# A transformer block on one core: second-matrix weights split once and kept, router steps respread, a prologue in another order

## The chip, the cores and the metric

The kernel runs on one core of one Trainium2 chip. The metric is the device time of one execution in microseconds (us); lower is better. The engines are TensorE (PE; its weight loads are listed as PEld), VectorE (DVE), ScalarE (ACT), GpSimd (POOL), and SyncE (SP), whose queue issues nearly all DMA transfers.

## What is computed

Eight batches of 512 tokens, width 512, all in float32: a cross-attention block, then a feed-forward block with a router.

```python
x = x + xattn(layernorm(x), ctx, ctx, mask, bias, Wq, bq, Wk, bk, Wv, bv, Wo, bo)   # 16 heads
z = layernorm(x)
...
r = clip(layernorm(z, ln_g, ln_b) @ router_W.T + router_b, -10, 10)     # 256 columns
phi, idx = top_k(softplus(r), 8)
Z = phi / (sum(phi) + 1e-6) * tanh(sum(phi))
h_lat = einsum('nd,nkd->nk', z, unit_rows(raw_U)[idx])
dyn = einsum('nk,nkd->nd', h_lat * Z, unit_rows(raw_V)[idx]) * gamma
static = gelu(z @ W1.T) @ W2.T                                          # 512 -> 2048 -> 512
x = x + static + dyn
```

## The kernel before

Three stages follow one another: `project` (projections), `attend` (attention), and `blend` (output projection, router, feed-forward). The change touches `blend` alone, which takes the second half of the time.

**Arithmetic.** A float32 matrix product is made of three passes of TensorE on rounded halves: high·high, high·low, low·high. So each operand needs a "high" copy (a rounding copy) and a "low" one (the operand less its high copy). The first matrix, W1, is loaded ready-made from a buffer in DRAM (`wf_d`). The second, W2, is loaded raw for each batch again, 16 blocks of 128x512: ScalarE makes the high half (`weight_high`, L1761) and GpSimd the low half (`weight_low`, L1369). GELU outputs are split by VectorE (`gelu_high`, L1601) and GpSimd (`gelu_low`, L1364).

**Pairs.** One batch is eight pairs (`unit(b, f)`, f = 0 to 7); a pair makes two blocks of 128 hidden columns, for 512 tokens, by seven products instead of eight (P1, P6, P2, P7, P5, P4, P3 in that order, each six matmuls of 256 columns, L1929). Between these matmuls stand those of the second matrix for earlier pairs (`down_pass`, L1952: 24 of 512 columns in a pair) as fill. The sums that turn products into hidden columns are made on the other engines while TensorE goes on:

- `c1` (ScalarE, L1784) copies P1 and must be done before P2 begins;
- `u2`, `u3` (VectorE, L1675 and L1679) must be done before P7 and P4 begin;
- `c22`, `c21`, `c12` (VectorE, L1684, L1687, L1691) before P3, the next P1, and the next P6;
- GELU in three parts on ScalarE: G11 (L1787) after P2, G2 (L1802) after c21, G12 (L1806) after c12.

**The router** of a batch is spread over its pairs, in code that is placed by hand behind those five sums (`behind_u2`, `behind_u3`, ...). `route_at(b)` is 1 in batch 0 and 0 later; at = f - route_at(b) is the router's step. At step 2: clipping, the eight largest, `soften` (absolute value and exponential) and `soften_more` (w = u + 1, L1751, and a logarithm, L1752), both on ScalarE. At 3: `small_part`, `large_part`, `alpha`. At 4: `weigh` (four multiply-and-sum of 256, L1527), `bound` (tanh), `gains` (four products of 256 into hl, L1541). At 5: `turn_h`, eight transposes of hl on TensorE behind P5, which need all of `gains`. In pair 4 of batches 1 to 6 GpSimd also adds a bias to the next batch's x (`add_bo`, L1337, four times).

ScalarE loads a function table (ACT_TABLE_LOAD) each time it goes from GELU to the exponential or logarithm and back. Each engine works through its own list in the written order; semaphores tie them.

**Prologue.** Ahead of the first pair stand the output projections of batch 0 and 1 (`project_out(m, t)`, L1827), sums over the router's weights (L1886 and L1889; they wait for GpSimd's scaling, L1377), transposes of the unit rows (L1895), the normalisation of batch 0 (`normalise`, L1445), its transposes (`turn_z`, L1821), the sums and low halves of those (`z_sums`, L1453 to L1458; `z_lows`, L1464), and the centring and splitting of the router's weights (L1586, L1411, L1413).

## Time and profile before

| what | value |
|---|---|
| median of 3 runs | 1843.02 us (1837.35 to 1844.26) |
| profiled execution, its time | 1840.77 us |
| profiled execution, its span | 1838.9 us |
| TensorE matmul busy | 1780.7 us, 97% |
| VectorE / ScalarE / GpSimd busy | 70% / 52% / 61% |
| mean granted TensorE clock | 0.993 of 2.4 GHz |
| HBM traffic | 281.42 MB read, 67.11 MB written |

The span runs from the first to the last instruction; the device time of the same execution is 1.9 us more. A share is busy time over the span.

### The profile page before, as it was taken

What the parts mean: (1) busy time and instruction counts of PE and PEld (TensorE: products, weight loads), DVE (VectorE), ACT (ScalarE), POOL (GpSimd) and SP (SyncE); (2) the same over time, 40 slices, a digit from 0 to 9 for tenths busy, and PEclk for the clock granted to TensorE, in tenths of its full rate; (3) what the DMA queues carried; (4) which work ended last, traced back from release to release, by engine and by line L of the source; (5) the groups of instructions that cost most, each with busy time, mean ns of one, the idle gap of its engine ahead of it and who ended that gap; (6) DMA issues with size and microseconds to landing.
All of it is one profiled execution on the core that took longest, in us unless ns stands there. A gap on an engine that the chain in (4) does not pass through costs nothing. (4 is left out here: it accounts for less than half of the span.)

```text
span 1838.9 us, 34319 instructions
## 1 busy us (share of the span) xinstructions
PE 1780.7 (97%) x11952; PEld 1373.1 (75%) x11952; DVE 1286.4 (70%) x2780; ACT 963.3 (52%) x2141; POOL 1121.0 (61%) x578
## 2 busy tenths in 40 slices
PE   9999999999999999998899999999999999999999
PEld 7888885555555555555788888788788887888888
DVE  7565568999999999997646566664655657646562
ACT  3322227999999999995243423433324234242342
POOL 1323258999999999995455445554645546545543
PEclk9999999999999999999899999999999999999999
DMA  8997999354445435413265755746648557375473
GB/s 328 312 334 241 336 332 356 118 171 153 137 150 173 139 127 196 138 48 135 88 191 152 257 144 166 246 133 205 197 120 259 149 159 241 115 252 162 139 216 115
DMA packets 219178, 350.79 MB, mean 191 GB/s; under 512 B 15232, under 2 KB 71168, under 8 KB 218496
## 3 DMA queue, kind: packets, MB, share of 16 engines
q1 hardware_dynamic: 215456, 335.48, 56.6%
q0 software_dynamic: 3264, 12.58, 1.8%
q8 instruction: 99, 1.62, 0.3%
q10 hardware_dynamic: 288, 0.52, 0.1%
q14 instruction: 71, 0.58, 0.1%
HBM read 281.42 MB, written 67.11 MB: 190 GB/s over the span
## 5 line engine op out<-in xcount | busy, mean ns | idle before, releaser
L1929 PEld LDWEIGHTS banks<-n_zo,n_w 128*128 128x128 f32 x2688 | 501.1, 190 | 106.4 <-DVE h_bias L1675 20.2
L1929 PE MATMUL banks<-n_zo,n_w 128*128 128x256 f32 x2688 | 539.4, 284 | 36.1 <-DVE h_bias L1675 17.6
L1364 POOL TENSOR_TENSOR n_g_l<-h_pos,n_g_h 128x512 fp32r<-128x512 f32 x128 | 198.7, 1553 | 432.0 <-DVE n_g_h L1601 432.0
L1952 PE MATMUL banks<-n_w,n_g_h 128*128 128x512 f32 x1024 | 384.7, 395 | 0.0
L1098 ACT ACTIVATE l_tiles<-l_tiles,l_small 128x512 f32<-128x512 f32 x376 | 267.2, 714 | 0.1
L1032 DVE CUSTOM_DVE_ANT_0 l_tiles<-banks,l_tiles 128x512 f32<-128x512 f32 x353 | 224.8, 687 | 25.7 <-PE banks L934 24.6
L945 PEld LDWEIGHTS banks<-ident,l_tiles 128*128 128x128 f32 x1524 | 163.2, 141 | 90.1 <-issue 70.5
L945 PE MATMUL banks<-ident,l_tiles 128*128 128x128 f32 x1524 | 207.4, 279 | 1.0 <-ACT a_pT L1076 0.9
L1952 PE MATMUL banks<-n_w,n_g_l 128*128 128x512 f32 x512 | 202.7, 396 | 0.0
L1952 PEld LDWEIGHTS banks<-n_w,n_g_h 128*128 128x128 f32 x1024 | 193.7, 189 | 8.1
L1369 POOL TENSOR_TENSOR n_w<-h_bias,n_w 128x512 fp32r<-128x512 f32 x128 | 175.0, 1367 | 36.8 <-ACT n_w L1761 36.8
L1039 DVE COPY a_pT<-banks 128x512 f32<-128x512 f32 x256 | 164.4, 683 | 4.4 <-PE banks L945 3.1
L1076 ACT ACTIVATE a_pT<-banks 128x512 f32<-128x512 f32 x256 | 151.5, 592 | 29.3 <-PE banks L945 24.7
L959 PE MATMUL banks<-a_pT,a_v 128*32 128x256 f32 x2048 | 149.9, 388 | 0.0
L1802 ACT ACTIVATE h_pos<-h_pos 128x512 f32<-128x512 f32 x64 | 40.5, 632 | 203.2 <-DVE h_pos L1687 203.1
L934 PE MATMUL banks<-h_k,h_q 32*128 32x512 f32 x1008 | 143.7, 639 | 2.8 <-PEq L162 1.0
L899 POOL TENSOR_TENSOR l_tiles<-a_pos,l_bias 128x2048 f32<-128x2048 f32 (+1 forms) x32 | 137.3, 4301 | 3.6 <-PE banks L945 3.3
L1787 ACT ACTIVATE h_pos<-banks 128x256 f32<-128x256 f32 x64 | 24.7, 386 | 163.9 <-PE banks L1929 163.9
L1675 DVE TENSOR_TENSOR h_bias<-banks,h_bias 128x256 f32<-128x256 f32 x64 | 27.0, 423 | 107.7 <-PE banks L1929 82.6
L1952 PEld LDWEIGHTS banks<-n_w,n_g_l 128*128 128x128 f32 x512 | 96.6, 189 | 5.3
L1679 DVE TENSOR_TENSOR h_bias<-banks,h_bias 128x256 f32<-128x256 f32 x64 | 26.7, 417 | 98.1 <-PE banks L1929 98.1
L1098 ACT ACTIVATE a_t_s<-a_t_s,l_small 128x512 f32<-128x512 f32 x128 | 91.5, 719 | 0.0
(254 smaller groups left out, 3684.7 us busy)
## 6 DMA issues: line engine op xcount, KB each, us to landing
n_w<-wf_d SPq DMA_DIRECT2D x448, 256.0 KB, 3.0
h_bias<-in_W2T SPq DMA_DIRECT2D x128, 256.0 KB, 3.3
a_pos<-pos_d SPq DMA_DIRECT2D x16, 1024.0 KB, 5.7
l_bias<-in_bias POOLq DMA_DIRECT2D x9, 1024.0 KB, 8.3
l_tiles<-in_x SPq DMA_DIRECT2D x8, 1024.0 KB, 10.4
l_bias<-in_mask SPq DMA_DIRECT2D x8, 1024.0 KB, 13.2
k_d<-l_tiles SPq DMA_DIRECT2D x8, 1024.0 KB, 11.6
pos_d<-l_bias SPq DMA_DIRECT2D x8, 1024.0 KB, 10.9
```

Of the source, the lines that this page charges most:

```text
L899: pool.tensor_tensor(out=t_s[j % NN][:, first:end, :], in0=pos_rows(b, qt, qt + 1).broadcast_to([P, end - first, S]), in1=bias_rows(first, ...
L934: pe.matmul(ps_s[:, i, :], q[rows, b, qt * P:(qt + 1) * P], k[rows, b, :], start=True, stop=True).then_inc(scored, 1)
L945: last = pe.transpose(ps_t[:, BANK[i], kt * P:(kt + 1) * P], t_s[at[1] % NN][:, i, kt * P:(kt + 1) * P], ident[:, :])
L959: last = pe.matmul(ps_o[rows, :], v[:, b, kt, rows], pT[:, h, i, kt, :], start=kt == 0, stop=kt == NT - 1)
L1032: dve.tensor_tensor_reduce(t_s[j % NN][:, i:i + 1, :], ps_s[:, i:i + 1, :], added, 1.0, 3.0e38, ALU.add, ALU.min, nmax[:, j % NN, i:i + 1] ...
L1039: dve.tensor_copy(dst, src).then_inc(kept_dve, 1)
L1076: act.activation(dst, src, ACT.Copy).then_inc(kept_act, 1)
L1098: act.activation(t_s[j % NN][:, i, :], t_s[j % NN][:, i, :], ACT.Exp, scale=-1.0, bias=nmax[:, j % NN, i:i + 1], accum_out=total[:, j // 2 ...
L1364: pool.tensor_tensor(out=g_l[:, j % NG, :], in0=g_f[:, j % NG, :], in1=g_h[:, j % NG, :].bitcast(F32), op=ALU.subtract).then_inc(g_low, 1)
L1369: pool.tensor_tensor(out=w2[:, j % NG, 1, :], in0=w2_raw[:, j % 2, :], in1=w2[:, j % NG, 0, :].bitcast(F32), op=ALU.subtract).then_inc(w2_ ...
L1929: last = pe.matmul(bank, w1[:, q % NR, m, k * P:(k + 1) * P], zo[:, j, MOVING[i], k, :], start=s == 0 and i in (P1, P6, P5), stop=s == NPP ...
L1952: last = pe.matmul(ps_y[:, t, :], (g_h, g_l)[i][:, j % NG, t * P:(t + 1) * P], w2[:, j % NG, k, :], start=f == 0 and m == 0, stop=f == NF ...
```

## The change

**Weights.** In batch 0 the split of W2 is made as before, and each split block (high and low, 512 KB) is written to a new DRAM buffer `w2_d` (16 writes). In batches 1 to 7 a block comes back from there with one load of 512 KB, straight into its place (`w2`), instead of a raw load of 256 KB, a ScalarE copy and a GpSimd subtraction. The loads wait for the block's last reader (`wait_used`), and one of a pair's two loads stands behind P5.

**Router.** `soften_more` moves from the end of step 2's pair to step 3, between G11 and G2; `small_part`, `large_part` and `alpha` move later; `weigh` is cut in two, behind u3 and behind c22 of step 4; `gains` is cut in two, behind c12 of step 4 and behind u2 of step 5; tanh goes behind G2.

**Prologue.** The last output projection of batch 0 and the transposes of the unit rows go ahead of the sums over the router's weights. VectorE normalises batch 0 before it takes up those sums. The residuals (1, 2) and (1, 3), the centring and the splits move from the front of the first pair into its gaps. ScalarE copies the transposed rows to SBUF (`u_raw`) first.

```diff
@@ SyncE
+                    if j < NF:
+                        need(sp, w2_low, j - 1)
+                        sp.dma_start(w2_raw[:, j % 2, :], W2T.rearrange("(f p) n -> f p n", p=P)[block_of(j)]) \
+                            .then_inc(w2_in[j % 2], 16)
+                    else:
+                        wait_used(sp, j - NG)
+                        sp.wait_ge(w2_out[j % 2], 16 * (NF // 2))
+                        sp.dma_start(w2[:, j % NG, :, :].bitcast(F32), w2_d[j % NF]).then_inc(w2_in[j % 2], 16)
+            def store_w2(j):
+                if 0 <= j < NF:
+                    sp.wait_ge(w2_low, j + 1)
+                    need(sp, w2_out[j % 2], 16 * (j // 2))
+                    sp.dma_start(w2_d[j], w2[:, j % NG, :, :].bitcast(F32)).then_inc(w2_out[j % 2], 16)
...
                     if i == 1:
-                        need(sp, w2_low, 2 * n)
+                        store_w2(2 * n - 1)
+                    if i == (1 if b == 0 else P5):
                         load_w2(2 * n + 1)
-                sp.wait_ge(w2_low, 2 * n + 1)
+                store_w2(2 * n)
                 load_w2(2 * n + 2)
@@ GpSimd, a pair
-                weight_low(2 * n)
+                if b == 0:
+                    weight_low(2 * n)
                 gelu_low(2 * n)
-                weight_low(2 * n + 1)
+                if b == 0:
+                    weight_low(2 * n + 1)
@@ VectorE, prologue
-            residual(0, 1)
-            att_low(1, range(NC))
             residual(0, 2)
+            att_low(1, (0, 1))
+            residual(0, 3)
+            moments(0)
+            att_low(1, (2, 3))
+            normalise(0)
             dve.wait_ge(rows_in, 16 * 4)
             dve.wait_ge(g_scaled, 2 * NC + NL)
             dve.wait_ge(g_summed, 2)
...
             residual(1, 1)
-            residual(1, 2)
-            residual(1, 3)
@@ VectorE, behind_u2 / behind_u3 / behind_c22 / behind_c21 / behind_c12
+                if b == 0 and f == 0:
+                    residual(1, 2)
+                    residual(1, 3)
...
-                if at == 3:
-                    small_part(b)
                 if at == 4:
-                    weigh(b)
+                    alpha(b)
+                if at == 5:
+                    gains(b, 2, NT)
...
+                if b == 0 and f == 0:
+                    centre()
...
-                if at == 3:
-                    large_part(b)
+                if at == 4:
+                    weigh(b, 0, 2)
...
+                if at == 3:
+                    small_part(b)
+                if at == 4:
+                    weigh(b, 2, NT)
+                    inverse(b)
...
                 if at == 3:
-                    alpha(b)
+                    large_part(b)
                 if at == 4:
-                    gains(b)
+                    gains(b, 0, 2)
@@ ScalarE, a pair
-                weight_high(2 * n)
+                if b == 0:
+                    weight_high(2 * n)
...
-                if at == 4:
-                    bound(b)
+                if at == 3:
+                    soften_more(b)
...
-                weight_high(2 * n + 1)
+                if b == 0:
+                    weight_high(2 * n + 1)
...
-                if at == 2:
-                    soften_more(b)
@@ TensorE, prologue
-            for t in range(NT - 1):
+            for t in range(NT):
                 project_out(0, t, 1)
+            pe.wait_ge(lat_unit, 2 + 2 * NL)
...
             pe.wait_ge(g_scaled, 2 * NC)
...
-            project_out(0, NT - 1, 1)
```

ScalarE's list in batch 1, from G2 of the pair of router step 2 on (h_bias<-banks is c1, h_pos<-banks is G11, h_pos<-h_pos 128x512 is G2 and 128x256 is G12). Before:

```order
L1802 ACT_TABLE_LOAD
L1802 ACTIVATE h_pos<-h_pos 128x512
L1806 ACTIVATE h_pos<-h_pos 128x256
L1761 ACTIVATE n_w<-h_bias 128x512
L1751 ACTIVATE n_w<-n_u 128x1024
L1752 ACT_TABLE_LOAD
L1752 ACTIVATE n_ln_w<-n_u 128x1024
L1784 ACTIVATE h_bias<-banks 128x256
L1787 ACT_TABLE_LOAD
L1787 ACTIVATE h_pos<-banks 128x256
```

In the changed kernel (its own line numbers):

```order
L1845 ACT_TABLE_LOAD
L1845 ACTIVATE h_pos<-h_pos 128x512
L1851 ACTIVATE h_pos<-h_pos 128x256
L1826 ACTIVATE h_bias<-banks 128x256
L1829 ACTIVATE h_pos<-banks 128x256
L1789 ACTIVATE n_w<-n_u 128x1024
L1790 ACT_TABLE_LOAD
L1790 ACTIVATE n_ln_w<-n_u 128x1024
L1845 ACT_TABLE_LOAD
L1845 ACTIVATE h_pos<-h_pos 128x512
```

c1 and G11 of the next pair now stand ahead of the identity and the logarithm, and the weight copy is gone.

VectorE's list in batch 1, from c12 of step 4's pair on (h_bias<-banks,h_bias is u2, then u3; h_q is hl). Before:

```order
L1691 TENSOR_TENSOR h_pos<-banks,h_bias 128x256
L1601 CAST n_g_h<-h_pos 128x512
L1537 TENSOR_TENSOR n_coef<-n_coef,n_tanh_s 128x4
L1541 SCALAR_TENSOR_TENSOR h_q<-n_sel,n_coef,h_q 128x256 x4
L1675 TENSOR_TENSOR h_bias<-banks,h_bias 128x256
L1601 CAST n_g_h<-h_pos 128x512
L1679 TENSOR_TENSOR h_bias<-banks,h_bias 128x256
```

In the changed kernel:

```order
L1729 TENSOR_TENSOR h_pos<-banks,h_bias 128x256
L1621 CAST n_g_h<-h_pos 128x512
L1560 TENSOR_TENSOR n_coef<-n_coef,n_tanh_s 128x4
L1564 SCALAR_TENSOR_TENSOR h_q<-n_sel,n_coef,h_q 128x256 x2
L1713 TENSOR_TENSOR h_bias<-banks,h_bias 128x256
L1621 CAST n_g_h<-h_pos 128x512
L1564 SCALAR_TENSOR_TENSOR h_q<-n_sel,n_coef,h_q 128x256 x2
L1717 TENSOR_TENSOR h_bias<-banks,h_bias 128x256
```

Two of the four products now stand behind u2 instead of ahead of it.

VectorE's list at the end of the prologue and in the first pair of batch 0 (n_ru and n_vg are split weights, k_x the residual stream, h_q the router's weights). Before:

```order
L1427 TENSOR_TENSOR k_x<-banks,k_x 128x512
L1430 BN_STATS n_stats<-k_x 128x6
L1586 TENSOR_TENSOR h_q<-h_q,h_pos 128x256 x4
L1411 CAST n_ru_h<-h_q 128x4x256
L1413 TENSOR_TENSOR n_ru_l<-h_q,n_ru_h 128x4x256
L1411 CAST n_vg_h<-n_w 128x1024
L1413 TENSOR_TENSOR n_vg_l<-n_w,n_vg_h 128x1024
L1675 TENSOR_TENSOR h_bias<-banks,h_bias 128x256
L1679 TENSOR_TENSOR h_bias<-banks,h_bias 128x256
```

In the changed kernel:

```order
L1713 TENSOR_TENSOR h_bias<-banks,h_bias 128x256
L1445 TENSOR_TENSOR k_x<-banks,k_x 128x512
L1448 BN_STATS n_stats<-k_x 128x6
L1445 TENSOR_TENSOR k_x<-banks,k_x 128x512
L1448 BN_STATS n_stats<-k_x 128x6
L1717 TENSOR_TENSOR h_bias<-banks,h_bias 128x256
L1604 TENSOR_TENSOR h_q<-h_q,h_pos 128x256 x4
L1722 TENSOR_TENSOR h_pos<-banks,h_bias 128x256
L1429 CAST n_ru_h<-h_q 128x4x256
L1431 TENSOR_TENSOR n_ru_l<-h_q,n_ru_h 128x4x256
L1725 TENSOR_TENSOR h_pos<-banks,h_bias 128x256
```

The first u2 now comes ahead of the residuals, the centring and the splits, which stand between the pair's five sums.

## Rows read from the trace of the kernel before

**Rows 1.** The page: the span.

```profile
span 1838.9 us, 34319 instructions
```

**Rows 2.** TensorE's waits: line, releaser, us in total, times, longest us.

```profile
PE banks L1929 <- DVE h_bias L1675: 17.6, 7, 5.9
PE banks L1929 <- ACT h_bias L1784: 10.6, 8, 1.3
PE banks L1929 <- DVE h_bias L1679: 8.0, 8, 1.0
```

**Rows 3.** TensorE's timeline, batch 2, pairs 2 to 5: start, length, idle time before.

```profile
1153.79 0.40 PE L1929 MATMUL banks<-n_zo,n_w 128*128 128x256 f32 x2
...
1164.32 0.40 PE L1929 MATMUL banks<-n_zo,n_w 128*128 128x256 f32 x2
...
1176.64 0.40 PE L1929 MATMUL banks<-n_zo,n_w 128*128 128x256 f32 x2
...
1188.47 0.40 PE L1929 MATMUL banks<-n_zo,n_w 128*128 128x256 f32 x2
...
1194.81 0.50 PE L1929 MATMUL banks<-n_zo,n_w 128*128 128x256 f32 x2 [1.94 <-DVE h_bias L1675]
...
1202.11 0.40 PE L1929 MATMUL banks<-n_zo,n_w 128*128 128x256 f32 x2
```

**Rows 4.** ScalarE's timeline, batch 2, between pairs 2 and 3.

```profile
1164.89 1.05 ACT L1751 ACTIVATE n_w<-n_u 128x1024 f32<-128x1024 f32 x1
1165.96 1.28 ACT L1752 ACT_TABLE_LOAD   x1
1167.25 1.06 ACT L1752 ACTIVATE n_ln_w<-n_u 128x1024 f32<-128x1024 f32 x1
1168.21 0.37 ACT L1784 ACTIVATE h_bias<-banks 128x256 f32<-128x256 f32 x1
```

**Rows 5.** VectorE's timeline, batch 2, pairs 4 and 5.

```profile
1182.21 1.50 DVE L1527 CUSTOM_DVE_ANT_0 n_sel<-n_w,n_sel 128x256 f32<-128x256 f32 x1
...
1183.64 0.41 DVE L1527 CUSTOM_DVE_ANT_0 n_sel<-n_w,n_sel 128x256 f32<-128x256 f32 x1
...
1188.61 5.81 DVE L1541 SCALAR_TENSOR_TENSOR h_q<-n_sel,n_coef,h_q 128x256 f32<-128x256 f32 x4
```

**Rows 6.** TensorE's timeline, prologue and first pairs of batch 0.

```profile
866.58 3.78 PE L1886 MATMUL banks<-h_q,ones 128*128 128x256 f32 x8 [5.56 <-POOL h_q L1377]
...
881.55 2.72 PE L1821 MATMUL banks<-ident,k_az 128*128 128x128 f32 x16 [2.68 <-DVE k_az L1445]
...
893.84 2.33 PE L1929 MATMUL banks<-n_zo,n_w 128*128 128x256 f32 x18
902.04 6.58 PE L1929 MATMUL banks<-n_zo,n_w 128*128 128x256 f32 x36 [5.88 <-DVE h_bias L1675]
...
908.46 0.40 PE L1868 MATMUL banks<-n_ru_h,n_zo 128*128 128x512 f32 x1
```

**Rows 7.** VectorE's timeline, prologue.

```profile
883.36 0.81 DVE L1453 TENSOR_TENSOR h_k<-h_k 128x512 f32<-128x512 f32 x1 [0.54 <-ACT h_k L1705]
...
888.46 2.48 DVE L1464 TENSOR_TENSOR n_zo<-banks,n_zo 128x512 fp32r<-128x512 f32 x4
...
895.45 1.41 DVE L1586 TENSOR_TENSOR h_q<-h_q,h_pos 128x256 f32<-128x256 f32 x4
```

**Rows 8.** GpSimd's timeline, prologue: the unit rows times gamma.

```profile
866.50 2.49 POOL L1380 TENSOR_TENSOR n_w<-n_sel,h_pos 128x512 f32<-128x512 f32 x2
```

**Rows 9.** The page's DMA issues: count, size of one, median us from issue to landing.

```profile
k_x<-in_x SPq DMA_DIRECT2D x8, 1024.0 KB, 8.2
```

**Rows 10.** Stretches: length, busy by engine, granted clock, DMA share, GB/s.

```profile
1137.80:1184.80 47.00, 44.72 (x268) 39.15 (x266) 26.14 (x58) 20.68 (x35) 23.80 (x16) 1.00 0.81 258
1073.00:1077.50 4.50, 4.07 (x16) 3.63 (x17) 3.24 (x6) 2.19 (x4) 4.50 (x4) 0.62 0.30 81
865.50:872.40 6.90, 5.82 (x14) 4.65 (x15) 1.61 (x3) 0.00 (x0) 3.49 (x3) 0.51 1.05 390
```

More of the change, by code:

```diff
@@ L66, in build @@
             attend(nc, ident, bias, q_d, k_d, v_d, pos_d, att_d, x, wo_d, bo, rawU, rawV, kept, ahead, late)
-        blend(nc, banks, ident, ones, neg_half, x, att_d, W2T, ln_g, ln_b, rWT, rb, gamma, wf_d, kept, ahead, out)
+        blend(nc, banks, ident, ones, neg_half, x, att_d, W2T, ln_g, ln_b, rWT, rb, gamma, wf_d, w2_d, kept, ahead, out)
 class Ahead:
@@ L83, in __init__ @@
             for n in ("pos_in", "q_out", "wf_out", "nbm_pool", "y_out", "passed"))
+        self.w2_out = [stack.enter_context(nc.semaphore(f"h_w2_out{n}")) for n in range(2)]
         self.w2_in = [stack.enter_context(nc.semaphore(f"h_w2_in{n}")) for n in range(2)]
@@ L1107, in _, with blend @@
             walk(act, step, 2)
-def blend(nc, banks, ident, ones, neg_half, x, att_d, W2T, ln_g, ln_b, rWT, rb, gamma, wf_d, kept, ahead, out):
+def blend(nc, banks, ident, ones, neg_half, x, att_d, W2T, ln_g, ln_b, rWT, rb, gamma, wf_d, w2_d, kept, ahead, out):
     UNITS = NF // 2
@@ L1648, in behind_c12 @@
                 at, m = f - route_at(b), b + 1
+                if b == 0 and f == 0:
+                    split(1, vg[0][:, :, :], vg[1][:, :, :], lat_vg[:, :, :])
                 if at in (0, 1):
@@ L1881, in _ @@
                 project_out(0, t, 0, 1)
-            for t in range(NT - 1):
+            for t in range(NT):
                 project_out(0, t, 1)
+            pe.wait_ge(lat_unit, 2 + 2 * NL)
+            for c in range(NC):
+                for n in range(NL):
+                    last = pe.transpose(ps_m[:, c // 2, (c % 2 * NL + n) * P:(c % 2 * NL + n + 1) * P],
+                                        u_dir[:, n, c * P:(c + 1) * P], ident[:, :])
+                if c % 2:
+                    last.then_inc(lat_turned, 1)
             pe.wait_ge(g_scaled, 2 * NC)
```

108 lines of the change are left out of this document (57 added, 51 removed).

## The prediction, made before the changed kernel had run

> **What bounds the kernel now.** I read the page first, for the span [rows 1] and TensorE's busy share in the table, then TensorE's waits, then its timeline at the places of those waits, then the timelines of the engine that ended each. The chain of waits runs through TensorE to the end. In `blend` TensorE's list is fixed by hand, and an undisturbed pair of batch 2 takes 1164.32 − 1153.79 = 10.53 us for 42 matmuls of 256 columns and 24 of 512 [rows 3]. So the change can gain only where TensorE waits or runs at the lower clock, and it removes no matmul. The waits are few and regular [rows 2]: once in each of 8 batches 1.3 us for c1 (ScalarE, L1784), once 1.0 us for u3 (VectorE, L1679), and 17.6 us in 7 times for u2 (L1675), of which 5.88 us in the prologue [rows 6], so six of 1.95 us in batches 1 to 6. The prologue has two more, 5.56 and 2.68 us [rows 6].
>
> What a wait costs is more than its idle time. From pair start to pair start, router step 2 to 3 costs 1176.64 − 1164.32 = 12.32 us, 1.79 over clean; step 4's pair 1188.47 − 1176.64 = 11.83, 1.30 over; step 5's pair 1202.11 − 1188.47 = 13.64 us [rows 3]. The last has eight transposes, about 1 us, so clean it would be 11.5, and 2.1 is lost. Batches 0 and 7 have the first two losses and no wait in step 5's pair.
>
> **Part 1, ScalarE (soften_more moved, weight copies gone).** Before, the identity, the table load and the logarithm stand ahead of the next pair's c1: 1.05 + 1.28 + 1.06 us, and c1 starts at 1168.21, 3.9 us into the pair, where P1 was done after 1.4 [rows 3, 4]. Now they stand between G11 and G2. Counted from the pair's start: G11 ends at 4.6, then 1.05 + 1.28 + 1.06 + 1.28 for the way back to GELU makes 9.3; G2 is due at 8.8 (c21). So G2 is 0.5 us late, and its reader is the fill of the next pair, some 7 us off. G12 comes at 10.2, c1 of the next pair at 11.9: on time. In batch 0 the copy `weight_high` adds two times 0.5 us, which still fits. The loss of 1.79 us goes, 8 times: **14.3 us**.
>
> **Part 2, VectorE at step 4 (weigh cut, small and large part and alpha moved).** A product of `weigh` takes 0.41 us clean and 1.50 while GpSimd works [rows 5]; four ahead of u3 made it late. Two now stand behind u3 and two behind c22. From the pair's start: u2 3.2, the GELU cast and `alpha` (1.2, as wide as `large_part`, estimated from the 1024-wide sums at 1.2) until 4.9, u3 due at 5.6, P4 needs it at 7.0. All fits, with c21 at 9.3 where the next P1 needs it at 10.5. The loss of 1.30 goes, 8 times: **10.4 us**.
>
> **Part 3, step 5 (gains cut).** The four products take 5.81 us, 1.45 each, because GpSimd's `gelu_low`, `weight_low` and `add_bo` alternate with them [rows 5]. Now two stand ahead of u2: from the pair's start 0.2 + 2 × 1.45 = 3.1, u2 ends at 3.5, P7 needs it at 4.2. So that wait of 1.95 goes. What is late next: `turn_h` on TensorE needs all four products. GpSimd no longer splits weights, so its four `add_bo` start at once and fill just this stretch. The GELU cast takes until 4.8, the other two products until 4.8 + 2.9 = 7.7, and P5 ends at 7.0. So 0.7 us of waiting, about 1.0 as lost time by the ratio in step 2's pair, and some 0.4 for c22, which stands behind two attention halves that wait for the same products. Of 2.1 us 0.7 is gained, in 6 batches: **4.2 us**.
>
> **Clock.** After two of the six 1.95 us waits the granted clock fell to the lower level, 1.2 GHz, for one stretch (0.62 as a mean over 1073.0 to 1077.5) [rows 10]. A 3.4 us stretch at half speed costs 1.7 us; without the waits two go: **3 us**.
>
> **Part 4, prologue.** Into the 5.56 us go nine matmuls of the last output projection of batch 0 (2.3 us, at about 0.23 each) and eight transposes (1.0): 2.3 remain. The 2.68 goes, since `normalise` no longer stands behind the router's sums. The next limit is on VectorE: g_mean waits for GpSimd's two products with gamma, 2.49 us [rows 8], and these now stand behind the first bias addition, which waits for x(1), issued at about 863 with 8.2 us to land [rows 9]. So 863 + 8.2 + 1.3 + 2.5 = 875. From there VectorE has 0.8 for g_mean and its row, 1.3 for a residual, 888.46 − 883.36 = 5.1 for `z_sums` and 2.48 for `z_lows` [rows 7]. The last projection needs the first half of `z_lows` (883.6) and takes 2.8: P1 of pair 0 at 886.5, before 893.84 [rows 6]. In pair 0 there is no fill, so VectorE's inserts show: residuals 2.8 ahead of u3, centring 1.41 [rows 7] ahead of c22, a split of about 2.2 ahead of c21, the direction's low half 1.3 ahead of c12. With 4 × 0.45 for the sums themselves, c12 comes at about 898.1 and the first router pass at 899, before 908.46 [rows 6]. That is 9.5 earlier. The short waits (1.3, 1.0, 1.6, 0.9) can bring the lower clock again, as 865.5 to 872.4 had it (0.51 [rows 10]); up to 2.3 us. I take **8.5 us**.
>
> **Part 5, weights.** Per pair 0.52 MB more is moved, in batch 0 1.05 MB of writes. Pairs 1 to 4 of batch 2 moved 258 GB/s at a DMA share of 0.81 [rows 10], so 318 GB/s at a share of 1. They hold 12.1 MB in 47.0 us; with 2.1 MB more in some 44 us they ask for 323 GB/s. That is just over, a backlog of 1 us at the end, or 3 in between, where the store and the load of x stand. It is hidden by the nine buffers of W1 blocks: nine products are 13 us, less a landing of some 3 us. If the cover were gone, each microsecond of backlog beyond 10 would be one of TensorE. The rows bound the rate at 390 GB/s from above [rows 10], where the backlog is none. SyncE's new waits for the last reader stand at the pair's end, 0.7 us, and ahead of P5's load, none. I cost all this at 0.
>
> The Trainium skill's page "DMA: Bandwidth & Descriptors" (section Specifications) puts the HBM limit of a core at about 358 GB/s. By it 14.2 MB would take 40 us and no backlog would arise; by the row's 318 GB/s, the stricter, 45 us. The stretch at 390 GB/s lies above the page's figure, so here the measurement decides.
>
> **Sum.** 14.3 + 10.4 + 4.2 + 3 + 8.5 = 40.4 us off the profiled execution's own 1840.77: **1800 us**. Its own time lies 0.12% under the median of the three runs, which is inside their spread.
>
> **Rivals.**
> (a) Likeliest, 0.78: as above. The lower end is step 5's wait gone too (6 × 1.4 = 8 us more), 1792; the upper is a prologue with lower clock and 4 us of gain, with step 5 no better than before, 1809.
> (b) The waits are only handed on, 0.12: the respread steps collide with other deadlines, for example c21 behind two `weigh` products and the reciprocal in batch 0, where GpSimd still splits weights, or u2 of step 4 behind `large_part` (2.2 us, ending 2.6 us into the pair). For it speaks that VectorE's two-input steps take 1.5 in place of 0.41 where GpSimd works [rows 5]; against it that GpSimd loses 14 subtractions in each of 7 batches. A new wait of 1.5 us in 8 batches takes back 12 us, and with a prologue at 4: 1817.
> (c) The transfers in batch 0 run short, 0.04: 1.8 + 0.5 + 1.05 MB in 10.5 us is 324 GB/s, and if writes cost twice what reads do, the backlog grows by some 2.4 us a pair and passes 10 us in pair 6. Price 5 to 8 us: 1807, inside the range.
> (d) Slower than before, 0.03: W1 blocks late in every batch. To lose more than the 40 us gained, pairs 1 to 4 must need 47.6 + 10 + 6 = 64 us of transfer instead of 46, that is a rate under 230 GB/s. The rows show 258 with room left, so only a collapse of the rate by the larger blocks would do it: 1850 and more.
> (e) The change does nothing in batches (the waits had another cause), 0.03: only the prologue, 1832.
>
> **How the numbers follow.** Faster by over 0.5% (9.2 us, about what a measurement here can tell from no change): all of (a), (b), (c) and most of (e), 0.94. Within: 0.03. Slower: 0.03. The range runs from 1791 to 1814 for (a), (c) and the better half of (b).
>
> **What would show it.** After: no wait of TensorE for c1 in any batch; none of 1.0 for u3; the u2 wait in pair 5 gone, and a wait of the transposes of hl for VectorE of 0.4 to 1.0 us in batches 1 to 6; clean pairs still 10.53 us; each batch from 1 on some 4 us shorter; first router pass near 899; no wait of TensorE for a DMA. Wrong would be: waits of L1972 (the changed product line) for W1 blocks, a DMA share at 1 over whole pairs with waits, or stretches at 1.2 GHz where TensorE did not wait before.

## The result and the profile after

The changed kernel takes 1799.11 us (median of 4 runs, 1797.42 to 1801.24), the kernel before 1841.92 us beside it (4 runs). The ratio is 0.9771, 95% interval 0.9749 to 0.9793, so some 42 us less. The prediction said 1800. One run of those below, of the kernel with the prologue alone, took 2361 us at a granted clock of 0.68 and is left out of its ratio.

From the page of the changed kernel, the span, the busy time by engine, and the DMA issues of the kept W2 blocks (count, size, us from issue to landing):

```profile
span 1795.6 us, 34021 instructions
PE 1769.6 (99%) x11952; PEld 1367.3 (76%) x11952; DVE 1247.0 (69%) x2779; ACT 905.8 (50%) x2030; POOL 971.5 (54%) x466
n_w<-w_d SPq DMA_DIRECT2D x112, 512.0 KB, 4.5
```

The span is 43.3 us shorter than in [rows 1]. The 112 loads of 512 KB are the kept blocks of batches 1 to 7. TensorE's waits from 850 us on (line, releaser, us in total, times, longest), against [rows 2]:

```profile
PE banks L1865 <- DVE k_az L1464: 3.7, 1, 3.7
PE banks L1972 <- DVE h_pos L1722: 1.8, 2, 1.1
PE banks L1865 <- DVE h_q L1564: 1.6, 6, 0.3
PE banks L1972 <- DVE h_pos L1725: 1.2, 1, 1.2
PE banks L1972 <- DVE h_bias L1717: 1.1, 1, 1.1
```

The eight waits for ScalarE are gone, and so are the eight for u3 of router step 4 and the six of 1.95 us for u2. What stands in their place in batches 1 to 7 is six waits of 0.3 us for the gains (L1564). The rest lies in the prologue and in batch 0: 1.1 us for u3 (L1717), 0.7 for c22 (L1722), 1.2 for c21 (L1725) in its first pair, where nothing fills TensorE's list, and 1.1 for c22 in its pair 5. No line names a DMA.

TensorE's timeline in batch 2 (start, length, idle time before): the starts of pairs 3, 4 and 5, the transposes of `hl`, and the start of pair 6. It answers to [rows 3].

```profile
1148.13 0.40 PE L1972 MATMUL banks<-n_zo,n_w 128*128 128x256 f32 x2
...
1158.66 0.40 PE L1972 MATMUL banks<-n_zo,n_w 128*128 128x256 f32 x2
...
1169.18 0.40 PE L1972 MATMUL banks<-n_zo,n_w 128*128 128x256 f32 x2
...
1176.65 1.09 PE L1865 MATMUL banks<-ident,h_q 128*128 128x128 f32 x8 [0.27 <-DVE h_q L1564]
...
1181.47 0.40 PE L1972 MATMUL banks<-n_zo,n_w 128*128 128x256 f32 x2
```

Pairs 3 and 4 now take 10.53 us each, the clean length, where they took 12.32 and 11.83. Pair 5 takes 1181.47 − 1169.18 = 12.29 where it took 13.64. Batch 2 is 4.5 us shorter as a whole. The prologue and batch 0 in the same view, against [rows 6]:

```profile
866.24 1.99 PE L1935 MATMUL banks<-h_q,ones 128*128 128x256 f32 x8 [0.59 <-POOL h_q L1393]
...
876.40 3.68 PE L1865 MATMUL banks<-ident,k_az 128*128 128x128 f32 x16 [3.67 <-DVE k_az L1464]
...
888.93 4.03 PE L1972 MATMUL banks<-n_zo,n_w 128*128 128x256 f32 x30
...
900.15 0.40 PE L1910 MATMUL banks<-n_ru_h,n_zo 128*128 128x512 f32 x1
...
949.09 0.40 PE L1972 MATMUL banks<-n_zo,n_w 128*128 128x256 f32 x2
...
958.80 0.51 PE L1972 MATMUL banks<-n_zo,n_w 128*128 128x256 f32 x2 [1.10 <-DVE h_pos L1722]
...
961.04 0.39 PE L1972 MATMUL banks<-n_zo,n_w 128*128 128x256 f32 x2
```

The first router pass is at 900.15, before it was at 908.46 [rows 6]. Pair 5 of batch 0 (949.09 to 961.04, 11.95 us) is the one pair with router step 4 that did not get shorter: it was 11.78.

**Where the 43.3 us came from.** All rows here are differences of starts in the two traces.

| place | us |
|---|---|
| pair with router step 3, 8 batches (1.80 to 1.84 each) | 14.6 |
| pair with step 4, batches 1 to 7 (1.22 to 1.30 each) | 8.8 |
| the same in batch 0 | −0.2 |
| pair with step 5, batches 1 to 6 (1.34 to 1.39 each), 0.2 in each of batches 0 and 7 | 8.6 |
| lower clock in that pair of batches 1 and 3 (15.2 us long before) | 3.1 |
| from the last transposes of the attention part to the first router pass (59.4 to 49.8 us) | 9.6 |
| the parts ahead of it, which the diff doesn't touch | −1.3 |

The parts that the diff doesn't touch end at 849.1 to 854.4 us in the fourteen traces of this study, so medians of two kernels can differ by some us without a cause in the edit. The pairs of batches 1 to 7 repeat to within 0.1 us from batch to batch where no lower clock falls into them. The effects below are therefore read from pairs, and the medians stand beside them.

### The profile page after: what moved, and what is told of

Same layout as the page of the kernel before. It is cut to its first block, busy times and chain, and to the rows that moved or that the text cites. A ratio compares the mean times of both kernels' runs of the same rounds, so it can differ in the third digit from the quotient of the medians.

```text
span 1795.6 us, 34021 instructions
## 1 busy us (share of the span) xinstructions
PE 1769.6 (99%) x11952; PEld 1367.3 (76%) x11952; DVE 1247.0 (69%) x2779; ACT 905.8 (50%) x2030; POOL 971.5 (54%) x466
## 4 chain that ended last, share of the span: by engine, by line
PE 46%; DVE 4%; issue 1%; ACT 0%; POOL 0%; DVEq 0%; ACTq 0%
PE banks L1998 18%; PE banks L1972 16%; PE banks L1871 7%; PE banks L1910 5%; DVE h_q L1564 2%; PE banks L1865 1%; DVE n_g_h L1621 1%; DVE n_aT_l L1438 0%; DVE k_x L1445 0%; ACT n_aT_h L1775 0%; DVE k_az L1464 0%; DVE n_stats L1448 0%; DVE h_pos L1722 0%; DVE k_x L1614 0%; DVE h_bias L1713 0%
## 5 line engine op out<-in xcount | busy, mean ns | idle before, releaser
L1972 PE MATMUL banks<-n_zo,n_w 128*128 128x256 f32 x2688 | 533.8, 282 | 5.3 <-DVE h_pos L1722 1.8
L1845 ACT ACTIVATE h_pos<-h_pos 128x512 f32<-128x512 f32 x64 | 40.4, 632 | 182.9 <-DVE h_pos L1725 182.7
L1717 DVE TENSOR_TENSOR h_bias<-banks,h_bias 128x256 f32<-128x256 f32 x64 | 26.8, 419 | 105.8 <-PE banks L1972 105.8
L1910 PE MATMUL banks<-n_ru_h,n_zo 128*128 128x512 f32 x256 | 90.3, 391 | 0.0
## 6 DMA issues: line engine op xcount, KB each, us to landing
l_tiles<-in_x SPq DMA_DIRECT2D x8, 1024.0 KB, 10.4
```

The costliest lines, as they stand in the source:

```text
L1910: last = pe.matmul(ps_m[:, t % 2, :], z_tokens(i, c, t), ru[j][:, c, :], start=s == 0, stop=s == NRP - 1)
L1972: last = pe.matmul(bank, w1[:, q % NR, m, k * P:(k + 1) * P], zo[:, j, MOVING[i], k, :], start=s == 0 and i in (P1, P6, P5), stop=s == NPP ...
```

## The experiments

**Theory:** each of the named waits was made by what stood ahead of the awaited instruction in its engine's list, so the respread removes the waits for c1 and u3, the cut of the gains those of pair 5, and the kept weights help only by taking GpSimd away from beside VectorE. **Rival:** the kept weights do most of it, since they take two ScalarE copies and two GpSimd subtractions out of each pair. The first four kernels apply or undo one part.

### Kept weights alone

The kernel before, with the SyncE, GpSimd and ScalarE part of the change.

```diff
...
+                    else:
+                        wait_used(sp, j - NG)
+                        sp.wait_ge(w2_out[j % 2], 16 * (NF // 2))
+                        sp.dma_start(w2[:, j % NG, :, :].bitcast(F32), w2_d[j % NF]).then_inc(w2_in[j % 2], 16)
...
-                weight_high(2 * n)
+                if b == 0:
+                    weight_high(2 * n)
```

> The kernel before with only the split weights of W2 written back in batch 0 and loaded in batches 1 to 7; router steps and prologue as before. Theory 1 (the router's new places remove the waits, as the prediction booked it; the kept weights are worth nothing by themselves): pairs of step 3 and 4 stay at 12.3 and 11.8 us, time within 3 us of before. Theory 2 (the waits were also made of ScalarE's two weight copies and GpSimd's splits): in batches 1 to 7 c1 comes 1.04 us earlier, so its wait falls from 1.3 to about 0.3 us, and the four products of step 4 no longer meet GpSimd's weight split (1.1 us earlier), so the wait of 1.0 us is gone; the wait of 1.95 us in step 5 stays. That is 2.8 us in 7 batches, 18 to 20 us less than before: about 1822.

Measured: 1832.27 us, ratio 0.9938 (0.9921 to 0.9956). TensorE's waits, and one stretch behind a wait of pair 5 (length, busy by engine, granted clock, DMA share, GB/s):

```profile
PE banks L1950 <- DVE h_bias L1692: 17.5, 7, 5.9
PE banks L1950 <- ACT h_bias L1803: 7.1, 8, 1.5
PE banks L1950 <- DVE h_bias L1696: 1.0, 1, 1.0
```

```profile
1193.80:1197.20 3.40, 3.40 (x13) 3.02 (x12) 2.12 (x4) 1.37 (x3) 1.48 (x2) 0.50 0.22 46
```

Pair 3 is 11.59 us instead of 12.33, since the wait for ScalarE falls from 1.3 to 0.8 (by the 0.5 us of one weight copy ahead of c1, not by the 1.04 of two that was expected); pair 4 is clean in batches 1 to 7, the 1.0 us wait is left in batch 0 alone; pair 5 is as long as before. So the kept weights alone remove, in batches 1 to 7, all of the step-4 loss and 0.74 of the 1.8 us of step 3. Of these 14 us 4 or 5 are lost again: the waits of 1.94 us in pair 5 were followed by 3.4 us at 0.50 of the clock in five batches here, in two before. That the kept weights help only through GpSimd, as the theory has it, does not hold for step 3: there it is ScalarE's copy that is gone.

### Without the kept weights

The changed kernel, with W2 split anew in every batch and no stores; router and prologue as changed.

```diff
-                if b == 0:
-                    weight_low(2 * n)
+                weight_low(2 * n)
...
-                if b == 0:
-                    weight_high(2 * n)
+                weight_high(2 * n)
```

> The changed kernel without the kept weights: W2 loaded raw and split in every batch; router steps and prologue as in the change. Theory 1 (router's places carry it): within 3 us of the changed kernel, 1799 to 1802. Theory 2 (what batch 0 of the changed kernel shows holds for every batch with GpSimd's weight splits): step 4's pair 11.9 us instead of 10.53 in 7 more batches, and step 5 no better than now: 10 to 14 us more than the changed kernel, about 1811.

Measured: 1809.57 us, ratio 0.982 (0.9798 to 0.9841). TensorE's waits in the batches:

```profile
PE banks L1958 <- DVE h_pos L1712: 8.0, 7, 1.2
PE banks L1851 <- DVE h_q L1554: 3.1, 6, 0.5
```

Pair 3 is 10.53 and pair 4 10.7 us. Pair 5 is 13.60 to 13.69, as before the change, but with other waits: 0.5 us for the gains and 1.2 us for c22. Pair 5 of batch 0, 11.95 in the changed kernel, is 10.76 here. So the respread alone removes the loss of step 3 and all but 0.2 us of that of step 4 in all eight batches; the kept weights are worth 0.2 us in pair 4 of seven batches and 1.35 us in pair 5 of six, and cost 1.2 us in batch 0.

### The prologue alone

The kernel above, with the router's steps put back.

```diff
                 if at == 4:
-                    alpha(b)
-                if at == 5:
-                    gains(b, 2, NT)
+                    weigh(b, 0, NT)
+                    inverse(b)
...
+                if at == 2:
+                    soften_more(b)
```

> The kernel before with only the new prologue (and the first pair's inserts); router steps as before, W2 raw in every batch. Both theories: 9.6 us less than before, 1832; the pairs of batches 1 to 7 as before (12.3, 11.8, 13.6 us). If the prologue's gain were handed back later in batch 0, less than 5 us.

Measured: 1831.02 us, ratio 0.9938 (0.9913 to 0.9962). The pairs of the batches are those of before (12.33 to 12.36, 11.79 to 11.83, 13.65 to 13.69 us), with the lower clock behind the wait of pair 5 in one batch (15.20 us). From the last transposes of the attention part to the first router pass it takes 49.6 us, before 59.4. The prologue is worth its 10 us by itself. The other traces agree: this stretch takes 59.4 and 59.5 us in the two with the old prologue, 47.0 to 50.7 in the ten with that of the changed kernel.

From pair 2 of batch 0 to the end it takes 918.6 us before the change, 917.2 with the prologue alone, 891.9 with the respread too, 883.6 in the changed kernel. Less one stretch of lower clock, the respread is worth 23.8 us in this order and the kept weights on top of it 8.3; taken first, the kept weights were worth 14 us before what the clock took back. So the rival, that the kept weights do most of it, does not hold, and they are not worth nothing either.

### The gains in one piece

```diff
-                if at == 5:
-                    gains(b, 2, NT)
...
-                    gains(b, 0, 2)
+                    gains(b, 0, NT)
```

> The changed kernel with the four products of the gains together ahead of u2 again. Theory: the wait of 1.95 us for u2 comes back in batches 1 to 6, step 5's pair 13.6 instead of 12.3 us, 8 us more than the changed kernel, and up to 3 more if stretches at 1.2 GHz follow the waits: 1807 to 1810. Rival (with GpSimd's weight splits gone the products are short enough anyway): no change.

Measured: 1807.92 us, ratio 0.9813 (0.9793 to 0.9834). The wait for u2 is back, six times:

```profile
PE banks L1970 <- DVE h_bias L1711: 11.6, 6, 1.9
```

Pair 5 is 13.65 us, with a stretch of lower clock behind it in two batches of six. With the last kernels this closes step 5: neither the cut alone (13.66) nor the kept weights alone (13.64) shortens that pair, both together do (12.29).

### The logarithms at their old place

```diff
-                if at == 3:
-                    soften_more(b)
...
+                if at == 2:
+                    soften_more(b)
```

> The changed kernel with one step put back: the logarithms of the gate (soften_more) stand again behind ScalarE's last GELU of the step-2 pair instead of behind its first GELU of the step-3 pair. My prediction gave that move 1.79 us a batch (14.3 us): by it the step-3 pair (pair 3, pair 4 in batch 0) goes back from 10.53 to 12.33 us and the time to about 1813. Rival: the kept weights freed VectorE of most of this wait, as the kernel with kept weights alone showed a step-3 pair of 11.59; then the pair is 11.6 us in batches 1 to 7, 12.3 in batch 0, and the time is near 1799 + 7 x 1.06 + 1.8 = 1808.

Measured: 1805.17 us, ratio 0.9798 (0.9782 to 0.9815).

```profile
PE banks L1972 <- ACT h_bias L1826: 7.6, 8, 1.9
```

Pair 3 is 11.59 us, as the rival had it, not 12.33; in batch 0, where the copies remain, that pair is 12.78 and the next one is 10.54. So in this kernel the move is worth 7 × 1.06 + 0.8 = 8.2 us by the pairs, not 14.3. The rest of the wait the kept weights would have taken, through the ScalarE copy that is gone (the expectation's "freed VectorE" names the wrong engine).

### GpSimd's or ScalarE's share of the weights' work

Two kernels give the engines work of the old kind and place back in batches 1 to 7, on a buffer that nothing reads then.

```diff
                 if b == 0:
                     weight_low(2 * n)
+                else:
+                    idle_low(2 * n)
...
+            def idle_low(j):
+                pool.wait_ge(w2_low, j)
+                pool.tensor_tensor(out=w2_raw[:, 0, :], in0=w2_raw[:, 1, :], in1=w2_raw[:, 1, :], op=ALU.subtract).then_inc(w2_low, 1)
```

> The changed kernel, with GpSimd subtracting one 128x512 buffer from itself at each place in batches 1 to 7 where it split a W2 block before; nothing reads the result. The transfers are those of the changed kernel. Theory: what the kept weights gave in the step-5 pair (12.29 against 13.64 us) they gave through GpSimd, whose work slows VectorE beside it. Then the step-5 pair is 13.6 again in this kernel and the time is near 1799 + 6 x 1.35 = 1807. Rival: it was ScalarE's weight copies, which stood ahead of the work that TensorE waits for; then the pair stays at 12.3 here and the time at 1799.

```diff
                 if b == 0:
                     weight_high(2 * n)
+                else:
+                    idle_high(2 * n)
...
+            def idle_high(j):
...
+                act.activation(w2_raw[:, 0, :], w2_raw[:, 1, :], ACT.Copy).then_inc(w2_high, 1)
```

> The changed kernel, with ScalarE copying one 128x512 buffer at each place in batches 1 to 7 where it copied a raw W2 block before; nothing reads the result. Theory (GpSimd is the cause): the step-5 pair stays at 12.3 and the time at 1799. Rival: ScalarE's copies were the cause, the step-5 pair is 13.6 and the time near 1807. If each of the two gives back a part, the two kernels show by their pairs which part is whose.

Measured: GpSimd's work back, 1802.71 us, ratio 0.9788 (0.9766 to 0.981); ScalarE's work back, 1799.11 us, ratio 0.9777 (0.9745 to 0.9808). With GpSimd's work pair 5 is 13.13 to 13.17 us, with ScalarE's 12.29 to 12.33. GpSimd's timeline, then VectorE's, then TensorE's at pair 5 of batch 2, with GpSimd's work back:

```profile
1170.71 1.22 POOL L1390 TENSOR_TENSOR h_bias<-h_bias 128x512 f32<-128x512 f32 x1
1171.90 5.76 POOL L1353 TENSOR_TENSOR k_x<-k_x,k_bo_r 128x512 f32<-128x512 f32 x4
```

```profile
1177.30 2.60 DVE L1446 TENSOR_TENSOR n_aT_l<-k_az,n_aT_h 128x512 fp32r<-128x512 f32 x2 [0.45 <-ACT n_aT_h L1783]
1179.82 0.41 DVE L1730 TENSOR_TENSOR h_pos<-banks,h_bias 128x256 f32<-128x256 f32 x1
```

```profile
1180.29 0.51 PE L1980 MATMUL banks<-n_zo,n_w 128*128 128x256 f32 x2 [1.20 <-DVE h_pos L1730]
```

c22 (L1730) is made 1 us later than in the changed kernel because the two halves of `att_low` ahead of it take 2.60 us instead of 1.51, with one more GpSimd instruction ahead of the additions, which moves GpSimd's next work beside them. So GpSimd carries 0.87 of the 1.35 us, ScalarE none. Neither kernel gives the other 0.5 us back; whether it is the order of both or the arrival of raw blocks was not tried.

### The bias additions one pair later

```diff
-                if f == 4 and more and b > 0:
+                if f == 5 and more and b > 0:
                     add_bo(b + 1, (b + 1) % 2)
```

> The changed kernel with GpSimd's two-microsecond bias additions of the next batch (add_bo) one pair later, at pair 5 instead of pair 4, so that the step-5 or the step-4 pair has them elsewhere. Theory: the 1.8 us that the step-5 pair still costs over 10.53 (12.29 measured, 11.43 in batch 7, which has no next batch) is partly VectorE's work slowed by GpSimd's additions and the h_pos and h_bias copies behind it; moving the additions out of the step-4 pair takes the step-5 pair to about 11.4, near 5 us over the six batches, 1794. Rival: the additions then meet the step-5 pair's own VectorE work (gains, h_lows, att_low) and the pair gets longer, 1799 to 1806.

Measured: 1795.68 us, ratio 0.9742 (0.9725 to 0.9758). TensorE at pair 5 of batch 2, then the first two of VectorE's gains, then GpSimd's additions:

```profile
1169.15 0.40 PE L1972 MATMUL banks<-n_zo,n_w 128*128 128x256 f32 x2
...
1176.19 1.04 PE L1865 MATMUL banks<-ident,h_q 128*128 128x128 f32 x8
...
1180.59 0.40 PE L1972 MATMUL banks<-n_zo,n_w 128*128 128x256 f32 x2
```

```profile
1169.30 1.93 DVE L1564 SCALAR_TENSOR_TENSOR h_q<-n_sel,n_coef,h_q 128x256 f32<-128x256 f32 x2
```

```profile
1182.43 5.68 POOL L1353 TENSOR_TENSOR k_x<-k_x,k_bo_r 128x512 f32<-128x512 f32 x4
```

Two products of the gains take 1.9 us instead of the 2.9 of the changed kernel (its rows are below). The transposes wait for nothing, and the pair is 11.43 us, the length it has in batch 7. That is 0.86 us in each of six batches, as expected, though the intervals of the two ratios still overlap; the four additions now stand in pair 6, where TensorE is busy and no wait appears.

### GpSimd's order in the prologue

```diff
-            root(0)
-            add_bo(1, 1, 0, 1)
             pool.wait_ge(lat_unit, 2 + 2 * NL)
             for n in range(NL):
...
-            add_bo(1, 1, 1, NT)
+            root(0)
+            pool.wait_ge(normed, NNORMED)
+            add_bo(1, 1)
```

> The changed kernel with GpSimd's prologue in another order: gamma products first, then the root, and the bias additions of batch 1 only once VectorE has normalised batch 0. Theory: the four normalising operations took 5.74 us instead of 2.86 because GpSimd worked beside them, so TensorE waited 3.67 us for the transposes of z and its clock fell for 6.8 us behind that; without GpSimd beside them they take about 2.9 us, the wait is under 1 us, no half-clock stretch follows, and the kernel gains 3 to 5 us, 1794 to 1796. Rival: the bias additions then come late, and the residual additions of batch 1 or the first spreads with them: no gain or up to 3 us lost.

Measured: 1793.92 us, ratio 0.9736 (0.9722 to 0.9751). VectorE's normalising and TensorE's wait for the router's scaled weights:

```profile
873.60 1.92 DVE L1464 TENSOR_SCALAR k_az<-k_x,n_mv,n_rstd 128x512 f32<-128x512 f32 x4 [2.16 <-POOL n_rstd L1358]
```

```profile
869.66 3.47 PE L1935 MATMUL banks<-h_q,ones 128*128 128x256 f32 x8 [4.07 <-POOL h_q L1393]
```

The same wait in the list of the kernel with the gains in one piece, whose prologue is that of the changed kernel:

```profile
PE banks L1933 <- POOL h_q L1393: 4.1, 1, 4.1
```

The normalising takes 1.92 us for its four operations instead of 5.74, but starts 3 us later, since GpSimd's root now stands behind the gamma products. The wait for the transposes is gone and the one for the router's scaled weights is 4.07 us instead of 0.59. That wait is not the edit's: the scaling (L1393) stands ahead of everything that was moved, and, counted from the attention part, started 3.1 us later, 2.4 of them because the load of `ln_b` landed later. The kernel with the gains in one piece, where nothing was moved, has the same wait and none for the transposes. From the attention part to pair 2 it takes 61.3 us here, 61.6 in the changed kernel, and 58.9 to 63.4 in the ten traces with the changed kernel's prologue. So the shorter normalising is shown, and neither a gain nor a loss of time by it. The median is 5 us below that of the changed kernel, but the profiled execution is the slowest of its four (1797.59 us, against 1797.42 for the changed kernel's), so the trace has no place for those 5 us, and the two intervals touch.

### Loads ahead of the stores in batch 0

```diff
+                    if i == (1 if b == 0 else P5):
+                        load_w2(2 * n + 1)
                     if i == 1:
                         store_w2(2 * n - 1)
-                    if i == (1 if b == 0 else P5):
-                        load_w2(2 * n + 1)
-                store_w2(2 * n)
-                load_w2(2 * n + 2)
+                if n < UNITS - 1:
+                    load_w2(2 * n + 2)
+                    store_w2(2 * n)
...
```

> The changed kernel with SyncE's stores of split W2 blocks in batch 0 issued behind the load of the next raw block instead of ahead of it. Theory: the 1.1 us wait for u3 in pair 5 of batch 0 comes from the stores: the 256 KB load of the next raw block queues behind a 512 KB store, ScalarE's weight copy waits 0.84 us for it, GpSimd's split then falls into the time of alpha and weigh on VectorE, which it slows. With the loads first that pair is 10.8 us as in the kernel without kept weights, and the time 1 to 2 us lower. Rival: the weight copy waits for buffers that matmuls or the stores themselves still read, and nothing changes: pair 5 of batch 0 stays near 11.9.

Measured: 1797.02 us, ratio 0.9747 (0.9725 to 0.9768). ScalarE's copy of a weight block in pair 5 of batch 0, in the changed kernel:

```profile
954.52 0.63 ACT L1801 ACTIVATE n_w<-h_bias 128x512 fp32r<-128x512 f32 x1 [0.84 <-DMA h_bias<-in_W2T]
```

and with the loads first, with VectorE's `alpha` and TensorE's wait:

```profile
952.28 0.62 ACT L1805 ACTIVATE n_w<-h_bias 128x512 fp32r<-128x512 f32 x1
```

```profile
952.24 1.22 DVE L1543 TENSOR_TENSOR n_w<-n_w,n_ln_w 128x1024 f32<-128x1024 f32 x1
```

```profile
956.72 0.51 PE L1976 MATMUL banks<-n_zo,n_w 128*128 128x256 f32 x2 [0.33 <-DVE h_pos L1726]
```

The copy waits no more, the GpSimd subtractions move out of the time of `alpha`, which takes 1.22 us instead of 2.31, and TensorE's wait falls from 1.10 to 0.33 us. That wait is for c22 (L1722, here L1726), not for u3 as the expectation has it: u3 and two products of `weigh` stand between `alpha` and c22. The pair is 11.16 us instead of 11.95. The theory holds for 0.8 of the 1.2 us that the kernel without kept weights was better by.

### More bytes in batches 1 to 7

```diff
...
+                        sp.dma_start(w2_raw[:, j % 2, :], W2T.rearrange("(f p) n -> f p n", p=P)[block_of(j)]) \
+                            .then_inc(w2_out[j % 2], 16)
```

> The changed kernel with 256 KB more loaded beside each kept W2 block in batches 1 to 7 (into a buffer that nothing reads there): 0.52 MB more a pair, twice the bytes that the change itself added over the raw block. Theory (prediction part 5, transfers hidden): the mean rate of a batch goes from 228 to 264 GB/s, the blocks in hand cover it, TensorE waits for no DMA, 1799 within 3 us. Rival (d): the three pairs at a DMA share of 0.92 to 1.01 have no room, 0.52 MB at 345 GB/s is 1.5 us a pair, four such pairs are 6 us a batch, and TensorE waits for n_w1 or n_w2 blocks: about 1799 + 7 x 6 = 1841, some of it less where the cover holds.

Measured: 1799.93 us, ratio 0.9768 (0.9743 to 0.9792). Stretches of batch 2 (length, busy by engine, granted clock, DMA share, GB/s): pair 3 and the whole batch in the changed kernel; then pair 3, pair 5 and the whole batch with the extra loads:

```profile
1148.20:1158.70 10.50, 10.50 (x68) 9.45 (x67) 4.94 (x10) 6.37 (x9) 3.49 (x2) 1.00 1.01 370
1111.05:1226.42 115.37, 114.98 (x673) 100.84 (x672) 66.13 (x127) 34.38 (x59) 39.79 (x27) 1.00 0.69 228
```

```profile
1148.20:1158.70 10.50, 10.50 (x68) 9.45 (x67) 4.42 (x11) 6.37 (x9) 3.49 (x2) 1.00 1.05 401
1169.20:1181.50 12.30, 12.03 (x78) 10.70 (x77) 10.79 (x19) 3.65 (x9) 8.43 (x6) 1.00 1.02 372
1111.05:1226.42 115.37, 115.00 (x674) 100.85 (x673) 66.13 (x128) 34.34 (x59) 39.75 (x28) 1.00 0.75 265
```

The queue now runs at a share above 1 for three pairs on end, at 372 to 401 GB/s, and all pairs of batches 1 to 7 have their lengths within 0.05 us. No wait of TensorE names a DMA. The bytes that the change added have as much room again.

### The three that helped, together

The additions of GpSimd one pair later, the loads ahead of the stores, and in the prologue the root first, then the gamma products, then the additions once batch 0 is normalised.

```diff
-            add_bo(1, 1, 0, 1)
             pool.wait_ge(lat_unit, 2 + 2 * NL)
...
+            pool.wait_ge(normed, NNORMED)
+            add_bo(1, 1)
```

> The three edits that helped or might help, together: bias additions of the next batch at pair 5, loads ahead of stores in batch 0, and in the prologue GpSimd's root, then the gamma products, then the bias additions only once batch 0 is normalised. Theory: the effects add, since they lie in different places: 6 x 0.86 = 5.1 us in the step-5 pairs of batches 1 to 6, 0.8 us in batch 0, and 1.5 to 3 us in the prologue because the normalising takes 3 to 4 us instead of 5.74; so 1799 - 8 = 1791 us, 1788 to 1793. Rival: the prologue only trades the wait for transposes of z against the wait for the router sums again, as with the gamma products first: then 1793.

Measured: 1791.98 us, ratio 0.9727 (0.9702 to 0.9752). VectorE's normalising, and TensorE's waits in the prologue:

```profile
874.24 3.85 DVE L1468 TENSOR_SCALAR k_az<-k_x,n_mv,n_rstd 128x512 f32<-128x512 f32 x4 [0.34 <-POOL n_rstd L1362]
```

```profile
878.15 1.97 PE L1869 MATMUL banks<-ident,k_az 128*128 128x128 f32 x16 [1.66 <-DVE k_az L1468]
...
887.17 0.51 PE L1875 MATMUL banks<-k_wo_h,n_g_h 128*128 128x512 f32 x1 [1.58 <-DVE n_zo L1487]
```

Pair 5 is 11.43 us in all of batches 1 to 6, and the step-4 pair of batch 0 is 10.72 instead of 11.95: 5.2 + 1.2 = 6.4 us. In the prologue the wait of 3.67 us becomes 1.66, and a new one of 1.58 stands before the last projection, since the additions now slow VectorE's sums instead. The first product of pair 0 comes 36.3 us behind the attention part instead of 38.6, but the lower clock from 898.0 us on, among the waits of pair 0, makes pair 1 15.9 us instead of 14.1, and pair 2 starts 61.6 us behind the attention part in both. In four of the ten traces with the changed kernel's prologue a stretch of lower clock fell there too. So the theory holds in the batches, and in the prologue neither it nor the rival is shown. This is the best kernel of the study beside the one with the gamma products first, from which its time can't be told apart. By the pairs it is 6.4 us better than the changed kernel.

## Why the prediction was right, point by point

Term by term it was 14.3, 10.4, 4.2, 3 and 8.5 us, and the traces give 14.6, 8.6, 8.6, 3.1 and 8.3: 40.4 predicted, 43.2 found. The forecast subtracts from the profiled execution, whose counterpart is 1797.42 us, so it is 3 us off. The two large errors go opposite ways, and in so far the closeness of the total is luck.

**Part 1 (c1, 14.3 us): right, 14.6 by the pairs.** The wait is gone in every batch and pair 3 is clean. The move is sufficient (the kernel without kept weights) but not all of it was needed: with the kept weights in place it is worth 8.2 us, since the kept weights alone take 0.74 us a batch of the same loss.

**Part 2 (u3 at step 4, 10.4 us): the mechanism right in batches 1 to 7, the size 1.8 us too large, nearly all in batch 0.** Batches 1 to 7 gave 8.8 us. In batch 0 the pair stayed at 11.95, where the step said "All fits, with c21 at 9.3". It fitted, but for 0.2 us, without the stores (10.76). With them the wait of 1.0 us for u3 is gone and one of 1.10 us for c22 stands in its place. VectorE's timeline in the changed kernel, batch 0, the operation `alpha` and the sum u3 behind it:

```profile
953.24 2.31 DVE L1539 TENSOR_TENSOR n_w<-n_w,n_ln_w 128x1024 f32<-128x1024 f32 x1
955.47 0.41 DVE L1717 TENSOR_TENSOR h_bias<-banks,h_bias 128x256 f32<-128x256 f32 x1
```

`alpha` was costed at its clean 1.2 us, and Part 5 costed the stores at 0. The stores delay the raw load, the load the copy, the copy GpSimd's subtraction, and this falls beside `alpha`; with the loads first 0.8 of the 1.2 us come back, and the other 0.4 stay open. That was half of rival (b), a collision in batch 0 where GpSimd still splits weights, but once and not in eight batches.

**Part 3 (step 5, 4.2 us): the mechanism right, the size 3.9 us too small.** The u2 wait of 1.95 us went and the transposes wait 0.27 us, predicted 0.4 to 1.0. Two products were costed at 2 × 1.45 = 2.9, which is what the first two took (the other two 2.94):

```profile
1169.32 2.98 DVE L1564 SCALAR_TENSOR_TENSOR h_q<-n_sel,n_coef,h_q 128x256 f32<-128x256 f32 x2
```

The last two end 7.4 us into the pair where the step had 7.7, and P5 ends at 7.2 where it had 7.0. The mis-sized term is the remaining loss. The step had 1.4 us left (0.7 of waiting priced at about 1.0, and 0.4 for c22); against the 11.43 us of batch 7 only 0.86 was left, against the estimated clean 11.5 some 0.8. GpSimd's additions carry all of this 0.86: moved away, the pair is 11.43. The step named the additions as what fills this stretch, and the kernel that moves them shows it.

**Clock (3 us): right, 3.1.** Both stretches at 1.2 GHz in the batches are gone with the waits ahead of them. Kept weights alone, with the waits left, had five. The prologue alone, with the waits of before, had one, so that two were there to be gained is in part chance.

**Part 4 (prologue, 8.5 us): the size right, 9.6 less 1.3 that the parts ahead of it took more, 8.3 in the span; the way there only in part.** The first router pass came at 900.15, predicted 899. The wait of 5.56 us fell to 0.59, where the step left 2.3. On the way two more things differed. "The 2.68 goes" is wrong: it grew to 3.67 us, because `normalise` now runs beside GpSimd's additions and products:

```profile
870.60 5.74 DVE L1464 TENSOR_SCALAR k_az<-k_x,n_mv,n_rstd 128x512 f32<-128x512 f32 x4 [0.34 <-POOL n_rstd L1358]
```

```profile
870.55 1.29 POOL L1353 TENSOR_TENSOR k_x<-k_x,k_bo_r 128x512 f32<-128x512 f32 x1
```

And the lower clock came with that wait, not with the short ones of pair 0: TensorE was idle from 872.7 to 876.4, and from 874.9 to 881.7 the granted clock was 0.50, the lower level:

```profile
874.90:881.70 6.80, 5.30 (x21) 4.91 (x22) 5.41 (x10) 2.78 (x5) 5.93 (x7) 0.50 0.15 54
```

The g_mean chain, which the step had as the limit at 875, ran at 876.3 behind the normalising. P1 of pair 0 came at 888.93 instead of the predicted 886.5. The four gaps of pair 0 were 1.05, 0.69, 1.22 and 0.49 us, a total of 3.5 where 4.8 was predicted, which gave part of it back. That the short waits can bring the lower clock was right as a possibility: the profiled execution was spared, four of the ten with this prologue were not. So the errors on this path cancelled, and that the sum met 8.5 is luck.

**Part 5 (weights, 0): right in batches 1 to 7, wrong by 0.8 to 1.2 us in batch 0.** The transfers of the batches are hidden with 0.52 MB a pair to spare, so the backlog argued from 318 GB/s was too strict: stretches ran at 370 GB/s at a share of 1.01, and 401 with more bytes asked for. The kept weights were not free of effect, though: the prediction gave their relief to GpSimd one mention in Part 3. They are worth 1.35 us a batch there, 0.87 of it through GpSimd.

The Trainium skill's page "DMA: Bandwidth & Descriptors" (section Specifications) has about 358 GB/s as a core's HBM limit. The measured 370 to 401 GB/s over pairs of 10.5 us are above it, so this trace does not agree, with one core running.

**The rivals.** (b) held once, in batch 0. (c), transfers short in batch 0, did not happen as priced: no backlog reached TensorE; but the stores' place in the queue did cost what is told above. (d) is refuted with twice the added bytes. (e) is refuted.

## What to carry to other kernels

When waits come from work that stands ahead of an awaited instruction, two cures (moving it, and taking away what slows it) overlap: apply each alone before adding their gains, since here either of them removed the step-4 wait in batches 1 to 7, while in step 5 only both shortened the pair. Count the other engine's instructions in the same stretch before pricing a VectorE operation at its clean length, and look for the additions that can stand in a pair without a deadline. A store that is "hidden" can still cost by its place in a queue: issue the load that somebody waits for first. And before reading a gain of few us in a stage, look how much that stage differs between traces of the same code: this prologue did by 4.5 us.

## What the runs showed of the hardware

VectorE slows beside GpSimd by whole GpSimd instructions. The gains' products took 1.45 to 1.5 us each beside GpSimd's 1.44 us additions and 0.47 to 0.48 clean (the second and third of batch 2 with the additions moved); the 1024-wide sum 2.31 against 1.22; and normalising 128x512, an operation with one tensor input, 1.44 us each beside GpSimd and 0.48 without it. GpSimd's own four additions took 1.44 us each beside the gains and 1.42 in pair 6. It goes the other way too: in the changed kernel GpSimd's `gelu_low`, started at 1158.77 while VectorE's 1024-wide `large_part` ran from 1158.61, took 2.21 us, and 1.29 at 1169.30. u2, which reads one operand from TensorE's banks, kept its 0.41 us amid the additions (1172.22). The Trainium skill's page "SBUF — State Buffer" (section Who interferes with whom) says that VectorE operations with two SBUF inputs, and `tensor_scalar` in its two-port mode, contend with GpSimd, and that whichever starts later is blocked for the whole instruction of the other; the trace agrees for the three kinds above, though it does not show in which mode the normalising ran.

Waits of 1.94 us were enough for the lower clock in some batches and not in others of the same kernel (2, 5, 1 and 2 of 6 in the four kernels that had them), each time for a stretch of 3.4 us that cost about 1.55 us. The wait of 1.2 us for c22 in six batches, without the kept weights, brought none; the waits of pair 0, of 1.2 us and less close together, did in four of ten traces. What decides it the traces do not show.
